# Crossing from the convolution to the paired tiles: the last channels' rows handed over in SBUF, TensorE kept multiplying while it waits, constants made on GpSimd

## The reference

```python
x = x + _L0(x, length, ...)        # per channel: a causal convolution of 1024 taps over positions,
                                   # for positions < length[b]; elsewhere the layer adds nothing
x = x + einsum('bct,bcd->bdt', x, weights[condition])     # mixes the 64 channels, one of 16 matrices per sample
x = x + (x @ base_weight.T + base_bias + (x @ A[a].T) @ B[a].T)      # 1024x1024, rank-16 adapter chosen per sample
x = x + (x @ W.T + ((x @ lora_A[l]) @ lora_B.T) * 0.5)    # 1024x1024, rank-32 adapter chosen per sample
```

## Time and profile before

| what | value |
|---|---|
| median of 3 runs | 1459.91 us (1458.21 to 1460.43) |
| the profiled execution, own time | 1456.56 us |
| its span, first to last instruction | 1454.8 us |
| TensorE busy | 1425.0 us, 98% of the span |
| weight loads, VectorE, ScalarE, GpSimd busy | 1324.4, 1129.2, 612.3, 98.2 us |
| DMA over the span | 271.95 MB, 187 GB/s |
| mean granted TensorE clock | 0.996 of full speed |

### The profile page before, as it was taken

How to read it: one execution, slowest core, us unless ns; L and a number is a source line. 1 busy time by engine, 2 the same in 40 slices (tenths; PEclk the granted TensorE clock), 3 DMA queues, 4 the chain that set the end, 5 groups by cost and what they waited for, 6 DMA issues and landing times.

```text
span 1454.8 us, 31507 instructions
## 1 busy us (share of the span) xinstructions
PE 1425.0 (98%) x9304; PEld 1324.4 (91%) x9304; DVE 1129.2 (78%) x2297; ACT 612.3 (42%) x1217; POOL 98.2 (7%) x184
## 2 busy tenths in 40 slices
PE   6999999999999996999999999999999999999998
PEld 5888899999999996989999999999999999999997
DVE  7984488888888885787777777777778778778775
ACT  4332366666566562333343343343343343333332
POOL 3313100000000000000000000000000000000000
PEclk9999999999999998999999999999999999999999
DMA  8041288888888877456456556556556545645652
GB/s 312 0 147 30 70 302 274 274 272 274 277 269 275 273 234 210 131 166 203 148 163 202 149 166 200 145 160 204 152 152 200 169 152 183 186 152 168 200 152 81
DMA packets 116787, 271.95 MB, mean 187 GB/s; under 512 B 23881, under 2 KB 60109, under 8 KB 114097
## 3 DMA queue, kind: packets, MB, share of 16 engines
q1 hardware_dynamic: 106572, 237.08, 53.8%
q10 hardware_dynamic: 10182, 34.46, 6.0%
HBM read 198.62 MB, written 72.85 MB: 187 GB/s over the span
## 4 chain that ended last, share of the span: by engine, by line
PE 93%; DMA 3%; DVE 2%; SPq 1%; issue 1%; ACT 0%; DVEq 0%; ACTq 0%
PE ps L1591 18%; PE ps L1584 15%; PE ps L1222 13%; PE ps L1583 11%; PE ps L1564 8%; PE ps L1135 8%; PE ps L1233 6%; PE ps L1600 4%; PE ps L1213 3%; PE ps L1121 2%; PE ps L1225 2%; PE ps L1144 2%; DMA out<-y_out 1%; PE ps L1575 1%; SPq L393 1%
## 5 line engine op out<-in xcount | busy, mean ns | idle before, releaser
L1583 PE MATMUL ps<-weights,xa 128*128 128x256 f32 x1152 | 322.0, 281 | 1.7 <-ACT y_out L1374 1.5
L1584 PE MATMUL ps<-weights,xa 128*128 128x352 f32 x1152 | 322.9, 322 | 0.0
L1591 PE MATMUL ps<-weights,xs 128*128 128x512 f32 x1152 | 291.2, 401 | 0.0
L1591 PEld LDWEIGHTS ps<-weights,xs 128*128 128x128 f32 x1152 | 207.0, 189 | 40.3
L1222 PE MATMUL ps<-toep,ut 128*128 128x512 f32 (+2 forms) x1152 | 226.7, 342 | 0.0
L1583 PEld LDWEIGHTS ps<-weights,xa 128*128 128x128 f32 x1152 | 217.4, 189 | 4.1 <-issue 2.6
L1584 PEld LDWEIGHTS ps<-weights,xa 128*128 128x128 f32 x1152 | 216.2, 188 | 1.4
L1222 PEld LDWEIGHTS ps<-toep,ut 128*128 128x128 f32 x1152 | 194.3, 189 | 16.6
L1350 ACT ACTIVATE a<-ps 128x512 f32<-128x512 f32 x128 | 76.5, 597 | 285.2 <-PE ps L1564 284.8
L1564 PE MATMUL ps<-m_gath,x_in 128*128 128x128 f32 x1024 | 137.3, 278 | 9.7 <-DVE x_in L1449 9.7
L1564 PEld LDWEIGHTS ps<-m_gath,x_in 128*128 128x128 f32 x1024 | 129.0, 194 | 12.6 <-DVE x_in L1449 10.2
(11 more groups left out here) (222 smaller groups left out, 2218.5 us busy)
## 6 DMA issues: line engine op xcount, KB each, us to landing
xt<-in_xt SPq DMA_DIRECT2D x64, 512.0 KB, 5.7
x_d<-yo SPq DMA_DIRECT2D x64, 512.0 KB, 2.9
x_nat<-in_x SPq DMA_DIRECT2D x64, 512.0 KB, 3.9
x_in<-x_d SPq DMA_DIRECT2D x64, 512.0 KB, 5.9
lags<-kern_d SPq DMA_DIRECT2D x63, 512.0 KB, 4.9
out<-y_out ACTq DMA_DIRECT2D x62, 512.0 KB, 6.0
tab<-a_d SPq DMA_DIRECT2D x128, 128.0 KB, 2.1
stack<-b_d SPq DMA_DIRECT2D x126, 128.0 KB, 4.0
```

What stands on the lines that cost most here:

```text
L1583: mm(acc[:, left, 0:HALF], x_part, w[:, 0:HALF], start=start, stop=end, skip_group_check=True)
L1584: ins = mm(acc[:, right, 0:HALF + KR], x_part, w[:, HALF:WIDE], start=start, stop=end, skip_group_check=True)
L1591: ins = mm(acc[:, bank], operand[:, a, i, :], plain(i, b, m), start=opens and i == a == b == 0, stop=i == K4 - 1 and a == 1, skip_group_ch ...
```

## The change

- **First tiles.** `x1_in` of the first pair is no longer loaded whole after all stores have landed. The rows of channels 0 to 61 are loaded while channels 62 and 63 are still being computed, in loads of 60 and 2 rows for each sample. The rows of channels 62 and 63 are copied from the result tiles `yo` straight into `x1_in` by small DMAs from SBUF to SBUF (`last_rows`, four for each channel). The store of channel 63 to DRAM moves into the second block.
- **SP's queue.** The register reads `ids` for the first pair move ahead of the last five channels' loads; the eight transfers of `load_stack` move from ScalarE's queue to SP's, between `load_c` and the second pair's `x_nat`.
- **TensorE.** `keep_clock` multiplies the identity by itself into a part of PSUM that nobody reads yet: 27 times at the start, 7 times at the end of the first block, 4 times at the start of the second.
- **Constants.** The ten instructions of `fix` move from VectorE to GpSimd, behind the `c_gath` constants, which now wait for the store of channel 63. GpSimd's first `gather` moves into the first block.

```diff
+            pe.wait_ge(consts, 2)
+            keep_clock(target("a3a"), WARM_START)
...
+            keep_clock(ps[0], WARM_END)
...
+            first_a, first_l = [ids(sp, 0, v, B) for v in range(2)], [ids(sp, 0, v, 2 * B) for v in range(2)]
...
-            channel(GROUPS - 1, UNROLL - 2, loads=False)
-            channel(GROUPS - 1, UNROLL - 1, loads=False)
             for u in range(2):
-                sp.wait_ge(x1_stored[u], count_in(GROUPS, 0, 2))
+                sp.wait_ge(x1_stored[u], stored_all - 16)
             for v in range(2):
-                sp.dma_start(x1_in[v][:], x1_rows[v]).then_inc(x1_landed[v], 16)
+                if v == 1:
+                    sp.wait_ge(conv_done, C - 1)
+                for b in range(2):
+                    for first, end in ((0, EVEN_ROWS), (EVEN_ROWS, C - 2)):
+                        sp.dma_start(x1_in[v][b * C + first:b * C + end], x1_d[2 * v + b, first:end]).then_inc(x1_landed[v], 16)
+
+            def last_rows(eng, c, v, landed):
+
+                for b in range(2):
+                    row = b * C + c
+                    eng.dma_start(x1_in[v][row:row + 1], yo[c % 2][2 * v + b:2 * v + b + 1]).then_inc(landed, 16)
...
+            sp.dma_start(x1_d[:, C - 1], yo[(C - 1) % 2][:]).then_inc(x1_stored[1], 16)
...
             for v in range(2):
+                load_stack(sp, v, a[v])
+            for v in range(2):
                 sp.wait_ge(chosen[v], 2)
                 sp.dma_start(x_nat[v][:], x_rows[2 + v]).then_inc(x_landed[v], 16)
...
+            pool.wait_ge(x1_stored[1], stored_all)
             for v in range(2):
...
-            for v in range(2):
-                load_stack(act, v, ids(act, 0, v, B))
+            act.wait_ge(x1_stored[0], stored_all)
+            act.wait_ge(row_landed, 64)
...
-                fix(nc.vector.memset(hrow[v][:], 0.0))
...
+            dve.wait_ge(small_fixed, 10)
+            dve.wait_ge(x1_stored[1], stored_all)
...
+            keep_clock(acc[:, S_LEFT], WARM_DENSE)
             for q in range(4):
                 quarter(0, q, FIRST_BANKS[q])
```

More of the change, by code:

```diff
@@ L345, in program @@
     gathered = [sem(f"gathered{v}") for v in range(2)]
[L346 removed]
+    gfixed, c_fixed, small_fixed = sem("gfixed"), sem("c_fixed"), sem("small_fixed")
     mixed, quarter_read = sem("mixed"), sem("quarter_read")
@@ L372, in over_pairs, with gather @@
             body(n, n == PAIRS - 1)
+    def gather(pool, n, v):
+        for b in range(2):
+            s = pool.value_load(index[0:1, bass.ds(4 * n + 2 * v + b, 1)], min_val=0, max_val=S1 - 1)
+            rows = slice(b * C, (b + 1) * C)
+            ins = nc.gpsimd.tensor_copy(m_gath[v][rows, b * C:(b + 1) * C], mix[rows, bass.ds(s, 1), :].squeeze(1))
+        ins.then_inc(gathered[v], 1)
+        pool.wait_ge(gathered[v], n + 1)
     def h_table(half, m):
@@ L388, in products_of, with keep_clock @@
         return ((M1, 0), (M2, 1)) if v == 0 else ((M5, 0), (M4, 1))
+    WARM_START, WARM_END, WARM_DENSE = 27, 7, 4
+    def keep_clock(to, count):
+        for _ in range(count):
+            nc.tensor.matmul(to[:, 0:P], ident[:], ident[:], start=True, stop=True, skip_group_check=True)
     def ids(eng, n, v, base_of):
@@ L630, in _ @@
                         p2_identity(p2_late[v], (3, 7)[v], in_late[v])
+            pool.wait_ge(toep_lo, C)
+            for v in range(2):
+                nc.gpsimd.memset(m_gath[v][:], 0.0).then_inc(gfixed, 1)
+            pool.wait_ge(gfixed, 2)
+            for v in range(2):
+                gather(pool, 0, v)
         @block.scalar
@@ L1277, in _ @@
             for v in range(2):
+                load_stack(sp, v, a[v])
+            for v in range(2):
                 sp.wait_ge(chosen[v], 2)
                 sp.dma_start(x_nat[v][:], x_rows[2 + v]).then_inc(x_landed[v], 16)
+            for u in range(2):
+                sp.wait_ge(x1_stored[u], stored_all)
             def stacks(n):
@@ L1312, in _ @@
         def _(pool):
+            pool.wait_ge(x1_stored[1], stored_all)
             for v in range(2):
[L1314 to L1327, removed]
+                pool.wait_ge(x1_landed[v], LANDED_FIRST)
             for v in range(2):
@@ L1333, in _, with fix @@
             pool.wait_ge(c_fixed, 2)
+            fixed = [0]
+            def fix(ins):
+                fixed[0] += 1
+                ins.then_inc(small_fixed, 1)
+                pool.wait_ge(small_fixed, fixed[0])
+            for v in range(2):
+                fix(nc.gpsimd.memset(hrow[v][:], 0.0))
+                fix(nc.gpsimd.memset(hc[v][:], 0.0))
+                for b in range(2):
+                    fix(nc.gpsimd.tensor_copy(hc[v][KS:KS + 2, b * C:(b + 1) * C],
+                                              ident[KS:KS + 2, KS + b:KS + b + 1].to_broadcast([2, C])))
+                fix(nc.gpsimd.memset(f(hs[v][KS:KS + 2, 1]), 1.0))
             def pair(n, last_one):
```

37 lines of the change are left out of this document (20 added, 17 removed).

## The result

The changed kernel took 1461.9 us in the median of 17 runs (1459.68 to 1465.42); the kernel before took 1458.1 us beside it on the same chip. The ratio is 1.0023, with a 95% interval of 1.0017 to 1.003: **slower by 0.23%, some 3.4 us** (3.8 by the two medians), where 1.6 us less was forecast. The profiled execution took 1463.7 us (span 1461.9, mean granted clock 0.994).

A forecast was written before the change was run, and what follows sets the result against it. TensorE, busy 98% of the span, was taken as the bound, with gains only where it waits or runs at half clock. −0.6 (start) − 3.0 (`turn`) + 2.0 (clock) = −1.6 us, from 1459.91 to 1458.3 us; range 1453.5 to 1461.5.

The forecast's parts named there:

- The hole's move: TensorE's 9.07 us hole after the convolution shrinks below 3 us; one of 6 to 8 us opens before the `turn`.
- `turn` 3.0 us earlier: Middle of M4: `turn` comes 3.0 us earlier, bounds 1.4 and 5.5, set by SP's issues ahead of second pair's `x_in`.
- The clock, +2.0: Behind the `turn`: TensorE's clock falls in the new hole and its restart costs 2.0 us, bounds 1.7 and 2.9.
- What costs nothing: Eight register reads ahead of channel 59's load, 4.5 us of SP's queue, just hidden; at worst TensorE waits 0.5 us once.
- The start, −0.6: Kernel's start: filler lets `d0` run at full clock, 0.6 us gained, bounds 0.6 gained and 2.2 lost.
- The rival of loads in time: Second pair's loads land in time: 1455.6 us, or 1449.8 if VectorE did not wait at all; chance 0.26.
- The late last store: Channel 63's store takes 7.8 us to land, `turn` 1.1 us later than before, 1462.4 us; chance 0.12.

The follow-up runs named there:

- stack_last: Changed kernel with only the first pair's eight `stack` transfers moved behind the second pair's `x_nat` and `x_in` in SP's queue; 1454.3 us, 0.9965 of the kernel before.
- stack_on_act: Changed kernel with the eight `stack` transfers and the register reads they need back on ScalarE's queue; 1456.36 us, 0.9982 of the kernel before.
- x_first: Changed kernel with the register reads in the preparation and both `load_c` and `load_stack` behind the second pair's `x_in`; 1452.0 us, 0.9945 of the kernel before.
- x_first_loop: Changed kernel with early reads, second pair's loads ahead of `load_c` and `load_stack`, and the 27 start filler calls in a hardware loop; 1446.66 us, 0.9926 of the kernel before.
- reads_early: Changed kernel with only the eight register reads moved from ahead of channel 59's loads to the preparation; 1460.88 us, 1.0017 of the kernel before.
- again: The changed kernel run once more without any edit; 1461.56 us, 1.0015 of the kernel before.
- no_filler: Changed kernel without its 27, 7 and 4 `keep_clock` calls; 1460.1 us, 1.0009 of the kernel before.
- before_again: The kernel before, unedited, profiled a second time; span 1456.7 us.
- start_filler_loop: Kernel before with only the 27 start filler calls added, in a hardware loop; 1457.31 us, 1.0 of the kernel before.
- x_first_no_start: Changed kernel with early reads, second pair's loads ahead of `load_c` and `load_stack`, and no start filler calls; 1448.07 us, 0.9932 of the kernel before.

## Why the prediction was wrong

**The hole's move: right.** The first quarter starts earlier and at full clock, the gap between the parts is below 3 us, a hole opens before the `turn`, VectorE stands in `choose` for `x_in`, and the clock is at half behind it. `stack_last`, `stack_on_act` and `x_first` take the wait away by three ways, and each time the time falls by about what the trace says (`stack_last`: 8.3 us by the trace, 7.3 by the median).

**"`turn` 3.0 us earlier": the step that failed.** It came 0.1 us earlier. Against channel 63's end, term by term (forecast, measured): four row copies 1.4, 2.4; block to block 0.4, 0.7; store landing 3.6, 3.05; GpSimd 0.9, 1.1; `c_gath` 3.8, 4.0; `stack` 3.7, 6.2; `x_nat` 0.9, 1.0. That makes 14.8 and 18.5 us to the issue of `x_in`. Landing (6.4, 5.8) and the way from `choose` to the `turn` (4.46, 4.43) were right. The two terms that were most off are the ones with no row at this place. The row copies cost 0.60 us each and not the 0.35 of SP's cheap issues. And eight issues cost 6.2 us where four had cost 1.8 in a quiet queue: six took 0.3 to 0.4 with gaps to 0.5, the last two 0.85 and 1.98. A better row was there: in the kernel before the other four of the eight followed from 602.93 to 606.00, 3.1 us, with a slow one among them, and both halves together give 4.8 us and not 3.7.

```profile
602.93 0.32 SPq L412 DMA_DIRECT2D stack<-b_d  x1
603.34 0.36 SPq L413 DMA_DIRECT2D stack<-b_d  x1
603.90 1.64 SPq L412 DMA_DIRECT2D stack<-b_d  x1
605.63 0.37 SPq L413 DMA_DIRECT2D stack<-b_d  x1
```

In `stack_last`, behind `x_in`, the same eight took 4.1 us (566.57 to 570.69), in `x_first_loop` 4.4. The bound of 0.5 us for a short issue was too low for this queue. The Trainium skill ("DMA: Bandwidth & Descriptors", "Issuing engines are not separate DMA queues") calls the sequencer's time to initiate usually small relative to the DMA. For one issue this trace mostly agrees: 0.3 to 0.4 us, where the load lands 5.8 us after its issue. Eight in a row, 6.2 us, take longer than that landing, and moving them out of the load's way was worth 0.3 to 0.6%; so the rule doesn't carry over to the sum.

**The clock, +2.0: about right.** From the `turn` to the second pair's M1 it took 16.11 us before and 17.63 after, so 1.5 us lost (1.8, 1.9 and 2.1 in `reads_early`, `again` and `no_filler`). That the clock would fall 4.7 us into a hole did not repeat: it fell about 2.4 us after TensorE's last product in the changed kernel, 3.8 in `no_filler`. Both holes were long enough for either.

**"What costs nothing", the reads: wrong.** The eight reads took 5.7 us of SP's queue (509.1 to 514.78), 0.71 each, where 0.56 and in all 4.5 had been counted "just hidden". TensorE lost 1.2 us, the bound had been 0.5. The estimate was built on medians, and some of the reads are slow ones, up to 0.749 us beside a median of 0.270. The Trainium skill ("DMA: Bandwidth & Descriptors", "Latency and other measured facts") gives a floor of about 0.6 us for such a read. The rows of the reads alone disagree (0.262 us at least); only with the register work between them does a read come to 0.71.

**The start, −0.6: nothing between the two profiles compared, about right in the mean.** In the changed kernel the filler ended at 10.65, 1.3 us short of `d0`, and GpSimd's low part came at 23.9, not 23.55; channel 0 began at 179.04, as in the first profile of the kernel before. But that profile is the earliest of its kind. In the five profiles with nothing added at the start channel 0 began between 179.04 and 180.21 (179.6 in the mean; 180.12 in `before_again`), in the seven with the unrolled filler between 178.65 and 179.31 (179.0), in the two with the loop at 178.60 and 178.76. So a gain of about 0.6 us is likely there, no larger than the scatter, and no median shows it by itself (`start_filler_loop` 1.0). The unrolled filler didn't even hold the clock each time: in `reads_early`, `x_first` and `stack_on_act` the gap ahead of `d0` was 2.1 to 2.4 us and `d0` took 12.7 us again.

**What no step held: the length of the program.** The 27 unrolled calls cost 0.14% alone, 2 us net of whatever they gain at the start, at a place 170 us behind them. This and the `turn` together are the miss. As a ledger: forecast −1.6; +2.9 for the `turn`; −0.5 for the clock; +2.6 for the filler at the start (2.0 lost where 0.6 gained was forecast); +0.7 for the reads (by two medians; 1.1 by the trace). That sums to +4.1 where 3.4 was measured (2.2 in `again`); terms from profiles and from medians are mixed in it, so no more is to be had from the difference.

**The rival of loads in time** was worth what it said, once the loads were in time: 10.1 us of gain had been worked out for a VectorE that doesn't wait, and `x_first_no_start`, whose VectorE doesn't, is 9.9 us faster (0.9932), with the `turn` 9.3 us earlier behind channel 63 (19.54 against 28.81). It took more than the rival said, though: `c_gath` behind the load and the reads early as well. The late last store didn't happen: it landed in 3.05 us.

## What to carry to other kernels

When a wait is removed, find the next instruction on the released engine that waits for data, and look where that data's load stands in its queue. Here some 7 us, half of what the best version gains on the changed kernel, hung on eight short issues that could as well stand behind the load. Price issues by the rows of a loaded queue, not of a quiet one, and put what is needed last at the queue's end.

Filler for the clock is better put in a loop: unrolled, it lengthens the program, and here that moved a transfer of the instruction queue onto loads that mattered. And compare more than one profile of each kernel: two profiles of the unchanged kernel differed by 1.1 us at channel 0 alone.

## What the runs showed of the hardware

- Where a 16 KB transfer of the instruction queue ran just ahead of an issue on SP, that issue took 1.2 to 1.6 us in place of 0.43, in eight profiles of eight, and in none of the seven where it ran 6 us later or more. Why it does so the traces don't show.
- Counted from channel 0's first product, that transfer ran 7.3 us later in the kernel before (186.3), 0.3 us later with 54 passes of unrolled filler (179.4), 0.4 us later with 108 waits (181.5), and 7.0 us later with the filler in a loop (185.6).
- 108 instructions that only wait kept TensorE from its first product until 13.3 us. If they began at 1.6, when `ident` was ready, that is 0.11 us each.
- Holes of 8.6 to 9.2 us (three profiles) and of 5.9 us at the `turn` brought the clock to half, 2.4 to 2.6 and 3.8 us after TensorE's last product. The one of 2.4 us between the parts, with eight passes of filler behind it, left the clock full in five profiles and brought it to half in three.
- At channel 3 the mean clock from 196 to 212 was 1.00 behind the five waits of 1.46 to 1.71 us, 0.89 behind eight of 1.82 to 3.10, and 0.79 behind 3.01 and 3.23. A wait of 3.01 us stands in both of the last groups.
